# Routing rows of a mixture-of-experts layer: one region per expert, placed tile by tile, against one packed list placed per two tiles

## What is computed

```python
x = x + tanh(g_xattn[0]) * film(layernorm(x), ctx)           # tanh attention over 77 context rows
x = x + tanh(g_ffn[0])   * linear(layernorm(x))              # with a folded low-rank term
x = x + tanh(g_xattn[1]) * attention(layernorm(x), ctx)      # 16 heads of 16
x = x + tanh(g_ffn[1])   * moe(layernorm(x))
# moe, E = 16 experts, each row goes to K = 4 of them:
topk_idx, tw = _route(x, router_w, bias)
combine = (jax.nn.one_hot(topk_idx, E) * tw[..., None]).sum(1)
h = einsum('td,edf->etf', x, gate_w);  u = einsum('td,edf->etf', x, up_w)
y = einsum('etf,efd->etd', silu(h) * u, down_w)
routed = einsum('etd,te->td', y, combine)
sh = silu(x @ sh_gate_w) * (x @ sh_up_w) @ sh_down_w         # shared expert, all rows
```

## Time and profile before

| | us |
|---|---|
| median of 3 runs | 1582.64 |
| lowest, highest | 1576.61, 1583.19 |
| the profiled execution | 1580.62, its span 1578.9 |
| mean granted TensorE clock in it | 0.928 of full speed |
| steps 4, 5, 6, 7 (from the copy of rho to the next) | 150.5, 155.9, 160.6, 161.3 |
| step 8, step 9, step 10 with the end of its units | 129.6, 116, 105 |

### The profile page before, as it was taken

How to read it: one execution, slowest core, us unless ns; L and a number is a source line. 1 busy time by engine, 2 the same in 40 slices (tenths; PEclk the granted TensorE clock), 3 DMA queues, 4 the chain that set the end, 5 groups by cost and what they waited for, 6 DMA issues and landing times.

```text
span 1578.9 us, 34591 instructions
## 1 busy us (share of the span) xinstructions
PE 1296.2 (82%) x11876; PEld 761.8 (48%) x11876; DVE 951.1 (60%) x2301; ACT 1080.9 (68%) x1781; POOL 529.8 (34%) x505
## 2 busy tenths in 40 slices
PE   5777787787688999998999899989997886898860
PEld 2212242333225554655475546554666575577750
DVE  7986647635743775387438854895468865223323
ACT  4998886777887899878987897769872441222220
POOL 1101121121453221425543445256434434404216
PEclk8878997999799999999999999999998997899995
DMA  7654502503122343454444553534346554669954
GB/s 214 224 195 114 125 1 67 139 1 86 68 86 74 96 122 87 102 167 134 142 113 128 147 145 112 141 96 155 100 128 187 155 134 129 174 183 237 258 172 120
DMA packets 234433, 207.59 MB, mean 131 GB/s; under 512 B 121945, under 2 KB 191137, under 8 KB 234273
## 3 DMA queue, kind: packets, MB, share of 16 engines
q1 hardware_dynamic: 210017, 160.29, 37.8%
q0 software_dynamic: 12288, 33.57, 6.5%
q10 hardware_dynamic: 11968, 11.54, 2.3%
HBM read 110.01 MB, written 70.16 MB: 114 GB/s over the span
## 4 chain that ended last, share of the span: by engine, by line
PE 48%; ACT 21%; DVE 18%; issue 7%; POOL 4%; DMA 1%; another core or an unknown queue 1%; SPq 0%; POOLq 0%; DVEq 0%; ACTq 0%
ACT tanh_tiles L1251 17%; PE psF L1020 8%; PE psE L866 6%; PE psE L868 5%; PE psE L867 5%; PE psY L866 3%; PE psY L868 3%; PE psY L867 3%; PE psF L866 2%; PE psF L867 2%; PE psF L868 2%; PE psF L872 2%; POOL work L852 2%; PE psF L1190 1%; DVE xn L1457 1%
## 5 line engine op out<-in xcount | busy, mean ns | idle before, releaser
L1251 ACT ACTIVATE tanh_tiles<-feat,text_bias 128x512 f32<-128x512 f32 x1232 | 774.3, 713 | 77.9 <-DVE feat L1627 58.2
L1020 PE MATMUL psF<-tanh_tiles,wslide 128*32 128x512 f32 x2464 | 367.6, 652 | 60.4 <-ACT tanh_tiles L1251 59.0
L1656 DVE TENSOR_TENSOR tile<-tile,psE 128x512 f32<-128x512 f32 x128 | 87.5, 683 | 165.2 <-ACT tile L1278 87.7
L799 POOL TENSOR_TENSOR hid<-tile,hid 128x512 f16<-128x512 f32 x76 | 88.4, 1164 | 231.8 <-ACT hid L1270 231.0
L823 POOL DMA_INDIRECT xs_rows<-xs,slot_i x128 | 127.5, 996 | 115.2 <-PE psF L1020 43.6
L1270 ACT CAST hid<-tile 128x512 f16<-128x512 f32 x128 | 78.5, 613 | 119.8 <-DVE tile L1656 114.0
L866 PE MATMUL psY<-down,hid 128*128 128x256 f16 x512 | 143.0, 279 | 18.5 <-issue 12.7
L1278 ACT ACTIVATE tile<-psE 128x512 f32<-128x512 f32 x128 | 75.6, 591 | 115.7 <-PE psE L868 65.6
L866 PE MATMUL psE<-xg,gate_hi 128*128 128x128 f16 x768 | 147.1, 224 | 7.7 <-issue 6.7
L866 PE MATMUL psE<-xg,up_hi 128*128 128x128 f16 x768 | 147.4, 221 | 6.4 <-issue 5.2
L867 PE MATMUL psE<-xg,up_hi 128*128 128x128 f16 x768 | 147.3, 221 | 6.3 <-issue 6.1
(11 more groups left out here) (311 smaller groups left out, 2840.9 us busy)
## 6 DMA issues: line engine op xcount, KB each, us to landing
down<-down_split SPq DMA_DIRECT2D x208, 256.0 KB
y_rows<-hid SPq DMA_DIRECT2D x52, 256.0 KB
xs_rows<-peakT SPq DMA_DIRECT2D x24, 512.0 KB, 6.6
y_rows<-tanh_tiles ACTq DMA_DIRECT2D x44, 256.0 KB
down_split<-hid SPq DMA_DIRECT2D x18, 256.0 KB, 3.3
xscan<-in_x SPq DMA_DIRECT2D x8, 512.0 KB, 5.8
x<-in_x SPq DMA_DIRECT2D x8, 512.0 KB, 5.2
w_lin<-w_split SPq DMA_DIRECT2D x15, 256.0 KB
```

The lines of the kernel that those rows point to most:

```text
L799: pool.tensor_tensor(hid_lo[:, n], tile[:, v.n % 2], hid_hi[:, n], ALU.subtract).then_inc(glo_done, 1)
L1020: last = pe.matmul(psF[32 * j:32 * j + 32, RHO, :], wslide[:, c, 31 - g:63 - g], tanh_tiles[:, st.at(SETS, 2 * g + c) % HRING, j], start=g ...
L1251: act.activation(tanh_tiles[:, n % HRING, j], feat[:, c], ACT.Tanh, bias=text_bias[:, c, col:col + 1]).then_inc(h_ready, 1)
L1656: dve.tensor_tensor(tile[:, n], tile[:, n], psE[:, (2 * v.n + 1) % 3], ALU.mult).then_inc(g_done, 1)
```

## The change

Every expert gets a region of its own in xs_rows, of 1024 rows (`CAP`, 8 blocks, all rows that two tiles can send to one expert), so a row's place there doesn't depend on how many rows other experts have, and a tile can be placed and scattered by itself. The steps:

- **Places.** `positions` and `place` run for one tile, in every step 2 to 9: PE at slot 16, DVE at slot 17. A group's second tile adds to its matmuls the sums of the first tile (four) and the totals of the group (eight). PE waits for `choose` and, since psF[1] is in use by the layer norm phase, for LN3 (`xn_ready`); LN3T waits for `place` to have read. `choose` moves from slot 4 to slot 13 (ranking on POOL from 0 to 8), but stays at 4 in steps 2 and 7. In step 9 all is at slots 1 and 2.
- **Scatters.** 16 per tile, four at each of slots 18, 21, 24 and 27 (step 9: two per slot, 4 to 11), with their own table `slot_x`.
- **Group.** `place_group` on DVE at slot 24 of steps 3, 5 and 7 (slot 3 of step 9): owners, ids, `slot_i`, `wk`. Results still go to packed y_rows, so these stay; a product on `fill` and additions turn a block's number into its place in the regions.
- **Loads.** The two blocks of a unit are no longer neighbours: two transposing DMAs a unit, from an address that SP reads from `ids`; a word holds two 7-bit numbers.
- **Zeros.** Each buffer has 16384 rows: 32 pieces each. Buffer 0 is filled at slots 0 to 31 of step 1, buffer 1 at every third slot of steps 2 and 3.
- **Plan.** Step 8 has 18 units instead of 16, group 3 starts at slot 30 of step 9 instead of 36, and the last unit stands at slot 45 of step 10 instead of 51.

```diff
-CHOOSE = 4
-PLACE = 4
-SCATTER = 6
-PIECES = 12
+CAP = 2 * TOK
+SUB = CAP // P
+PIECES = 32
-        for u in range(18 if s > STEPS else 16):
+        for u in range(18 if s >= STEPS else 16):
-            g = now if s % 2 == 0 or u >= 12 else behind
+            g = now if s % 2 == 0 or u >= (6 if s > STEPS else 12) else behind
+def choose_slot(s):
+    return 1 if s > STEPS else 4 if s in KV_AT else 13      # KV_AT is steps 0, 1, 2, 7
+def position_slot(s):
+    return 2 if s > STEPS else 16
+def group_slot(s):
+    return 3 if s > STEPS else 24
 def scatter_slot(n, s):
-    return SCATTER + (n // 4 * 3 if s < STEPS else n // 2)
+    return 4 + n // 2 if s > STEPS else 18 + n // 4 * 3
...
-                    sp.dma_start_transpose(xg[:, v.r % XGRING], xs_dram[v.g % 2][v.pair * 2 * P:(v.pair + 1) * 2 * P, :]).then_inc(
-                        xg_loaded[v.r % XGRING], 16)
+                    word = sp.value_load(ids[0:1, v.g % 2, v.pair:v.pair + 1])
+                    for b, at in enumerate(blocks_of(word)):
+                        rows = blocks[bass.ds(sp.snap(at, min_val=0, max_val=E * SUB - 1), 1)].rearrange("o p n -> (o p) n")
+                        sp.dma_start_transpose(xg[:, v.r % XGRING, :, b * P:(b + 1) * P], rows).then_inc(
+                            xg_loaded[v.r % XGRING], 16)
-                if s in (1, 2) and i % 4 == 0 and i // 4 < PIECES:
-                    zero_piece(s - 1, i // 4)
+                if s == 1 and i < PIECES:
+                    zero_piece(0, i)
+                if s in (2, 3) and i % 3 == 0 and i // 3 < PIECES // 2:
+                    zero_piece(1, (s - 2) * (PIECES // 2) + i // 3)
...
-                g = place_due(i, s)
-                if g is not None:
-                    pe.wait_ge(sel_ready, 2 * g + 2)
-                    positions().then_inc(pos_ps, 1)
+                if ex and i == position_slot(s):
+                    pe.wait_ge(sel_ready, ex.at(1, 1))
+                    if st:
+                        pe.wait_ge(xn_ready, st.at(3, 2))
+                    else:
+                        pe.wait_ge(score_ready, STEPS)
+                    positions(ex).then_inc(pos_ps, 1)
...
                 if i == LN3T:
                     pe.wait_ge(xn_ready, st.at(3, 2))
+                    if ex:
+                        pe.wait_ge(pos_read, ex.at(1, 1))
...
+                last = dve.tensor_tensor(dest[:, mine], psF[:, 1, 0:width].rearrange("p (c e) -> p c e", c=NT),
+                                         region[:, :].unsqueeze(1).to_broadcast([P, NT, E]), ALU.add)
+                last.then_inc(pos_read, 1)
...
+                pl.link(dve.tensor_tensor(fill, fill, spare[0:1].unsqueeze(1).to_broadcast([1, BLOCKS, E]), ALU.mult))
                 pl.link(dve.tensor_reduce(owner, fill, AX, ALU.add))
```

More of the change, by code:

```diff
@@ L383, in build @@
         lows = work[:, p0 + 128:p0 + 384].rearrange("p (e f) -> p e f", e=E)
-        dest = work[:, p0 + 384:p0 + 512].rearrange("p (c e) -> p c e", c=CHUNKS)
-        share, nblk, first, past = (work[:, p0 + 512 + E * n:p0 + 512 + E * (n + 1)] for n in range(4))
+        dest_y = work[:, p0 + 384:p0 + 512].rearrange("p (c e) -> p c e", c=CHUNKS)
+        nblk, first, past, spare = (work[:, p0 + 512 + E * n:p0 + 512 + E * (n + 1)] for n in range(4))
+        pick_x = work[:, 2752:2752 + TOPK * NT * E].rearrange("p (k c e) -> p k c e", k=TOPK, c=NT)
+        slot_xf = work[:, 3008:3008 + NT * TOPK].rearrange("p (c k) -> p c k", c=NT)
+        share = work[:, 3024:3024 + E]
         slot_f = work[:, p0 + 576:p0 + 608].rearrange("p (c k) -> p c k", c=CHUNKS)
@@ L515, in run, with routed_tile, blocks_of, owners_of @@
                 slot(i, LAST + 1, None, None)
-        def place_due(i, s):
-            g = (s - 3) // 2
-            return g if i == PLACE and s % 2 and 0 <= g < GROUPS else None
+        def routed_tile(s):
+            return Tile(s - 2) if 2 <= s < STEPS + 2 else None
+        def blocks_of(word):
+            return [(word >> (7 * b)) & (E * SUB - 1) for b in range(2)]
+        def owners_of(word):
+            return [(word >> (7 * b + 3)) & (E - 1) for b in range(2)]
         def chunk_due(i, s, lag):
@@ L854, in _ @@
             run(None, slot)
+            pool.wait_ge(places_ready, GROUPS)
             for m, count in enumerate(group_stored(GROUPS - 1)):
@@ L995, in down_part, with positions @@
                 last.then_inc(y_ps, 1)
-            def positions():
-                chosen = sel[:, :, :].rearrange("p c e -> p (c e)")
-                width = CHUNKS * E
-                pe.matmul(psF[:, 1, 0:width], before[:, :], chosen, start=True, stop=False)
-                for c in range(1, CHUNKS):
-                    pe.matmul(psF[:, 1, c * E:width], ones[:, :], chosen[:, 0:width - c * E], start=False, stop=c == CHUNKS - 1)
-                for c in range(CHUNKS):
-                    last = pe.matmul(psF[:, 1, width:width + E], ones[:, :], sel[:, c], start=c == 0, stop=c == CHUNKS - 1)
+            def positions(ex):
+                mine = sel[:, ex.half * NT:(ex.half + 1) * NT].rearrange("p c e -> p (c e)")
+                width = NT * E
+                last = pe.matmul(psF[:, 1, 0:width], before[:, :], mine, start=True, stop=False)
+                for c in range(1, NT):
+                    last = pe.matmul(psF[:, 1, c * E:width], ones[:, :], mine[:, 0:width - c * E], start=False,
+                                     stop=ex.half == 0 and c == NT - 1)
+                if ex.half:
+                    for c in range(NT):
+                        earlier = sel[:, c].unsqueeze(1).to_broadcast([P, NT, E])
+                        pe.matmul(psF[:, 1, 0:width].rearrange("p (c e) -> p c e", c=NT), ones[:, :], earlier, start=False,
+                                  stop=c == NT - 1)
+                    for c in range(CHUNKS):
+                        last = pe.matmul(psF[:, 1, width:width + E], ones[:, :], sel[:, c], start=c == 0, stop=c == CHUNKS - 1)
                 return last
@@ L1659, in slot @@
                     dve.tensor_copy(rhoT, psF[:, RHO]).then_inc(rhoT_ready, 1)
-                if 2 <= s < STEPS + 2 and i == CHOOSE:
-                    ex = Tile(s - 2)
+                ex = routed_tile(s)
+                if ex and i == choose_slot(s):
                     dve.wait_ge(ranked, ex.at(1, 1))
                     choose(ex)
-                g = place_due(i, s)
-                if g is not None:
-                    place(g)
+                if ex and i == position_slot(s) + (0 if s > STEPS else 1):
+                    place(ex)
+                if ex and ex.half and i == group_slot(s):
+                    place_group(ex.batch())
                 due = chunk_due(i, s, add_lag)
```

97 lines of the change are left out of this document (58 added, 39 removed).

## The result

The changed kernel takes 1618.45 us (median of 4 runs, 1616.1 to 1621.55) against 1582.91 (the kernel before, now 4 runs): a ratio of 1.0235, 95% interval 1.0205 to 1.0266. It is slower, as forecast, by 36 us where the forecast said 12 to 14, and outside the range that was given. The profiled execution has a span of 1619.6 us (1578.9 before).

A forecast was written before the change was run, and what follows sets the result against it. PE was taken to bound steps 5 and 7, with steps 9 and 10 held by something else. Terms 18.5 + 4 + 21 - 11 - 14 + 13 - 8 - 11.5 + 2.5 = +14.5 on 1580.6 gave 1595 us, range 1568 to 1615.

The forecast's parts named there:

- the slack of steps 2 and 3: Slot 16 of steps 2 and 3: PE has slack there, so its wait for LN3 was taken as nothing.
- `place` at nothing: DVE at slot 17: eight short instructions per tile ahead of LN3T at slot 18, taken as 0.
- Positions at slot 16, 18.5 us: Steps 2 to 8: PE waits for LN3, which choose delays; 6.5 + 12 = 18.5 us, low 6, high 22.
- Clock, 4 us: Behind new PE waits over 4 us at slot 16: PE runs at a lower clock; +4 us, bounds 0 and 10.
- `place_group` at slot 24, 21 us: Steps 3, 5, 7: PE waits 5.1 us each for DVE's maxima, plus half clock; +21 us, low 6, high 27.
- slot 4's return, 11: Steps 5 and 7: PE no longer waits at slot 4 for choose and DVE's burst; -11 us, bounds 4 and 14.
- Scatters, -14: Steps 3, 5, 7: half as many scatters at a time shorten stalls; -14 us (8, 4, 2), bounds 0 and 20.
- Steps 9 and 10, -19.5: Step 9: thinner scatters recover PE idle time, -8 us; step 10: two units fewer, -11.5; bounds -28 and -12.
- Transfers, 2.5: More transposes and zero pieces on SP, +1, and repeated position matmuls, +1.5: +2.5 us, bounds 0 and 8.
- Partly absorbed: Rival: PE's waits cost half (20 of 43.5 us), gains stay at two thirds; 1587 us, no change; chance 0.24.
- The wait at slot 24 goes on: Rival: the fourth block's wait pushes q, scores and probabilities past their slots; 1624 us; three slower rivals together 0.14.
- The change doesn't thin the scatters: Rival: scatters now meet the maxima, so without gains of 14 and 8, 1617 us; three slower rivals together 0.14.

The follow-up runs named there:

- f2: The changed kernel as it is, run on the fourth chip beside three other kernels: 1.0235 of the kernel before.
- f3: Same kernel as e6 (choose, positions and place at slot 4, place_group at 24), run on the fourth chip: 1.0035 of the kernel before.
- e6: The kernel of e2 with only place_group moved to slot 24, on the second chip: 1590.35 us, 1.0027 of the kernel before.
- e2: The changed kernel with choose, positions, place and place_group all back at slot 4, rest of the change kept: 1590.08 us, 1.0006 of the kernel before.
- f1: The kernel before, unchanged, run as an experiment on the fourth chip for its trace: 0.9992 of itself.
- e8: The kernel before with the new plan of units alone, packed list and places as before: 1586.7 us, 1.0016 of the kernel before.
- e3: The changed kernel with place_group at slot 19 instead of 24: 1619.69 us, 1.0196 of the kernel before.
- f4: Same kernel as e10 (choose at slot 4, positions at 16 without the wait for LN3), run on the fourth chip: 1.0073 of the kernel before.
- e10: The changed kernel with choose at slot 4 and positions at 16 waiting only for the bank's last reader, third (fast) chip: 1.014 of the kernel before.
- e4: The changed kernel with step 8's 16 scatters at slots 36 to 45 instead of 18 to 27: 1624.05 us, 1.0226 of the kernel before.
- e7: The kernel of e2 with the scatters of steps 6 and 8 behind the gathers, slots 43 to 52: 1589.06 us, 1.0016 of the kernel before.
- g1: The kernel of f4 with the scatters of steps 6 and 8 at slots 43 to 52, fifth chip: 1586.37 us, 0.9999 of the kernel before.

## Why the prediction was wrong

The direction and the two kinds of wait were right, the size was not: +14.5 us was summed, and +36 measured. The steps that failed are the slack of steps 2 and 3, `place` at nothing, step 6 left out, and the units of step 10. By its terms:

- **Positions at slot 16, 18.5 us.** Right mechanism, mis-sized: 30.1 us of waits. The step that failed is "Steps 2 and 3 have slack on PE, and I take nothing": they have 4.1 and 6.0 us of wait, and f2 against f3 says that they pay for it (4.1 and 8.9 us; 3.7 and 4.2 of it between LN3 and the query product). Their PE has idle time, but not at that point: in step 3 of the kernel before, the chain of work that ended last runs through LN3's last instructions on DVE (444.22) and the transposes on PE behind them (445.77). Step 6 had 7.1 where I had 3.2. Steps 4 and 5 had 2.8 each where I had 4.2 and 4.5.
- **`place` at nothing.** "I take 0, since two slots lie between" is the second failed step. In step 3 the transposes (L909) began at 450.35, 5.4 us after LN3 ended at 444.98; before they began at once. PE's timeline in the changed kernel, the other position matmuls and a unit's gate products left out:

```profile
445.12 0.21 PE L1038 MATMUL psF<-sel,before 128*128 128x64 f16 x1 [6.04 <-DVE xn L1504]
...
445.77 1.94 PE L1063 MATMUL psF<-tanh_tiles,wslide 128*32 128x512 f32 x8
...
449.35 1.06 PE L1063 MATMUL psF<-tanh_tiles,wslide 128*32 128x512 f32 x8
450.35 1.09 PE L909 MATMUL psF<-ident,xn 128*128 128x128 f32 x8
```

  and in the kernel before:

```profile
445.77 1.97 PE L872 MATMUL psF<-ident,xn 128*128 128x128 f32 x8 [2.66 <-DVE xn L1457]
```

  It isn't the two slots or DVE's instructions (they end at 447.5) that cost. The kernel before did its tanh and unit matmuls first and waited for LN3 at slot 18, where only the transposes need it. The changed one waits at slot 16, and all the work between 16 and 18 (4.6 us; the scan's first eight matmuls took 1.94 us, the next eight 1.06, and the granted clock averages 0.77 from 445.1 to 452.0) comes after LN3 and ahead of its transposes. Where the chain through LN3 sets the step, that is what counts, and not how long PE stands: in step 3 f2 reaches LN3 2.8 us later than f3 after LN2 (`choose`) and the query product 4.2 later after LN3, 7.0 of the 8.9; in step 2, where `choose` stays at slot 4, it is 0.9 and 3.7. Where PE sets the step, the wait counts once: 2.8, 2.8 and 1.3 us in steps 4, 5 and 7 for 2.4, 3.2 and 1.2 more.
- **Clock, 4 us.** Over the seven us behind the waits of 4.1, 6.0, 7.1 and 6.2 us (steps 2, 3, 6 and 8) the granted clock averages 0.58, 0.77, 0.79 and 0.60; behind those of 2.8, 2.8 and 1.3 us (steps 4, 5 and 7) it is 1.00. In step 3 the kernel before is at 0.62 in that place too. No experiment parts the clock from the waits.
- **`place_group` at slot 24, 21 us, and slot 4's return, 11.** The waits came as worked out, 6.5, 6.5 and 6.0 for 5.1. But as a pair the terms should nearly have cancelled: e6 against e2 puts the net at 0.2% of the time, 3 us for my 10. The burst of 9 us on DVE costs several us at slot 4, 19 or 24 alike. Against the kernel before, f3 has 4.3 us more in step 5 and 0.5 in step 7.
- **Scatters, -14.** Step 3 gave 10.4 us in f3 (8 in the sum; place_group's leaving slot 4 is in it), steps 5 and 7 nothing on balance. What failed is that step 6 isn't in the sum at all, though it has the same gathers of the group before as step 8. f3 against f1 has it 13.4 us longer: 5.0 before LN3 begins, where no scatter has been issued yet and PE waits 7.3 us at slot 4 for `choose`, which the kernel before didn't need there, and 8.7 from the query product to the last maximum, beside the scatters. In step 8, 14.7 us longer (I had 13), the same two parts have 1.9 and 12.0.
- **Steps 9 and 10, -19.5.** Measured -11.8 (tail, f2 against f1). Fewer units aren't the reason: in the kernel before, in e8 and in all kernels with the change 37 of DVE's unit products lie in the tail, since the two units added to step 8 stand at its slots 48 and 51, behind LN4. Step 10's first and last product did come 8.7 us nearer each other (1564.58 - 1474.43 = 90.2 for 98.9), but "in step 10 two units fewer, so -11.5" took away work that only moved to the end of step 8; e8 shows the plan at nothing. What did shrink with the tail is the wait of DVE's product for a "remote": 22.9 us in f1, 32.0 in e8, 10.6 in f3 (26.9 and 10.8 in the first traces of the kernel before and the changed one). The thinner scatters of step 9 would explain that, but no run has them alone. With step 8 the tail makes +8.5 us for my -6.5.
- **Transfers, 2.5.** Not measured by itself: e2 has it together with gains and losses of 13 us and more. What there is fits: step 4, where f3 adds the doubled loads, the positions and 16 scatters, is 0.5 us longer than in f1, and step 1 with its 32 zero pieces is no longer, although a piece took SP 1.93 us (median) and not 0.93.
- **A slip in the rivals.** "Partly absorbed" leaves 20 of 43.5 us of waits, but its sum takes off 22, not 23.5. It decides nothing.

Of the rivals none was the result. "The wait at slot 24 goes on" had the right size (1624) and a wrong reason: e3 and e6 refute it. "The change doesn't thin the scatters" (1617) had part of the reason, in steps 6 and 8. The rule of the Trainium skill that stood with it ("SBUF — State Buffer", section "SBUF: two separate sides": GpSimd can't write its DMAs' descriptors beside DVE's two-port instructions) finds no support in the traces: in f4's stall DVE is busy only 6.3 of 28 us, and in the changed kernel the 128 scatters have a median of 971 ns, 12 above's minimum. That is the time of the issue; when the rows of a scatter had landed isn't in these numbers.

Still open is how PE, ACT and DVE come to stop together beside a row of indirect DMAs, and why they do so on one chip and hardly on another (f4 and e10, one kernel). That the stalls follow the scatters (e4, e7, g1) is shown; whether it is data, descriptors or the fetching of instructions isn't. No run took the transfers away while leaving the issues, or the reverse.

## To carry to other kernels

When an instruction needs a shared buffer, make it wait for the last reader of that buffer, not for the end of the phase that used it; and when a wait moves up in an in-order queue, ask what sets the length at that point: if it is the waiting engine, charge the wait; if it is the chain through the awaited thing, charge to it the work between the old place of the wait and the new one, which was done meanwhile before. An engine's idle time in a step says nothing on slack at one point of it. Work moved between stages of a schedule that is full has to be priced at both ends, and each added stage that runs "per tile instead of per group" has to be laid beside everything that already runs in the steps that had none.

## What the runs showed of the hardware that was not expected

- In f4 28 us in which POOL issues indirect DMAs back to back (about 1 us each and 0.3 between) and PE, DVE and ACT together are busy 13.5 us, with waits of 8 to 15 us without a visible sender, while the 16 DMA engines are full for the first 12 us (share 1.02, 226 GB/s) and a third busy for the rest (0.33). The same kernel on another chip (e10) was busy 44.0 us on the three engines in 28 us of the same row, with a DMA share of 0.76.
- One program on the five chips of the experiments: the kernel before has medians of 1541, 1584, 1586, 1587 and 1588 us. Ratios moved less, but not nothing: f4's kernel had 1.0073 on one chip and 1.014 on the fast one, with intervals that hardly meet.
